# Two pairs of stores made one DMA each, and the last rows' x loaded in sixteen small DMAs on ScalarE's queue (dropout, adjacency product, layer norm, one Trainium2 core)

## What is computed

```python
def reference(x, adj, u):                       # x, u: (8192, 64); adj: (8192, 8192), fp32
    keep = (u >= 0.1).astype(x.dtype)
    x_drop = x * keep / (1.0 - 0.1)
    y = x + jnp.matmul(adj, x_drop)
    m = jnp.mean(y, axis=-1, keepdims=True)
    v = jnp.var(y, axis=-1, keepdims=True)
    return (y - m) / jnp.sqrt(v + 1e-5)
```

## Time and profile before

| | |
|---|---|
| median of 3 runs | 643.01 us (642.99 to 643.07) |
| the profiled execution | 643.25 us, its span 641.5 us |
| granted TensorE clock, mean | 0.927 of full speed |
| TensorE busy | 514.2 us, 80% of the span |
| VectorE, ScalarE, GpSimd busy | 48.6, 10.8 and 18.0 us |
| moved by DMA | 274.80 MB, mean 428 GB/s over the span |

### The profile page before, as it was taken

How to read it: one execution, slowest core, us unless ns; L and a number is a source line. 1 busy time by engine, 2 the same in 40 slices (tenths; PEclk the granted TensorE clock), 3 DMA queues, 4 the chain that set the end, 5 groups by cost and what they waited for, 6 DMA issues and landing times.

```text
span 641.5 us, 5637 instructions
## 1 busy us (share of the span) xinstructions
PE 514.2 (80%) x2308; PEld 175.9 (27%) x2308; DVE 48.6 (8%) x230; ACT 10.8 (2%) x18; POOL 18.0 (3%) x27
## 2 busy tenths in 40 slices
PE   0397888778988797797788779788797788689796
PEld 0132223222222232232232223222232232223225
DVE  2100101010010100101010010100001010000102
ACT  0000000000000000000000000000000000000000
POOL 0000000000000000000000000000000000000000
PEclk9998888998979798898989989798898989989999
DMA  9999999999999999999999999999999999999998
GB/s 374 423 448 436 429 432 440 416 440 425 430 436 450 412 449 440 429 426 443 413 440 429 430 432 454 426 432 443 423 430 439 420 437 447 428 416 428 434 422 335
DMA packets 9962, 274.80 MB, mean 428 GB/s; under 512 B 1388, under 2 KB 1642, under 8 KB 2666
## 3 DMA queue, kind: packets, MB, share of 16 engines
q1 hardware_dynamic: 9660, 274.60, 99.5%
q10 hardware_dynamic: 300, 0.16, 0.1%
HBM read 272.66 MB, written 2.10 MB: 428 GB/s over the span
## 4 chain that ended last, share of the span: by engine, by line
DMA 70%; PE 27%; issue 1%; SPq 0%; DVE 0%; POOL 0%; POOLq 0%; ACT 0%; DVEq 0%
DMA raw<-adj_dram 70%; PE acc L173 26%; SPq L132 0%; PE turned L193 0%; POOL rstd L268 0%; DVE stats L238 0%; POOLq L47 0%; ACT sums L211 0%; DVE rows L234 0%; SPq L137 0%; SPq L135 0%; SPq L136 0%; DVE moments L243 0%; POOLq L273 0%; DVE final_normed L261 0%
## 5 line engine op out<-in xcount | busy, mean ns | idle before, releaser
L173 PE MATMUL acc<-raw,dropped 128*64 128x504 f32 x2048 | 488.5, 637 | 93.3 <-POOLq L273 89.3
L173 PEld LDWEIGHTS acc<-raw,dropped 128*64 128x64 f32 x2048 | 152.9, 147 | 417.2 <-issue 291.5
L234 DVE TENSOR_TENSOR rows<-turned,x_sb 126x256 f32<-126x256 f32 x16 | 6.8, 425 | 541.8 <-PE turned L193 541.8
L268 POOL TENSOR_TENSOR rstd<-var_eps,minus_half 126x4 f32<-126x4 f32 x16 | 16.2, 1013 | 613.4 <-DMA raw<-adj_dram 330.2
L193 PE MATMUL turned<-join,sums 128*126 128x64 f32 x128 | 17.5, 279 | 10.9 <-ACT sums L211 10.9
L193 PEld LDWEIGHTS turned<-join,sums 128*126 128x126 f32 x128 | 15.3, 189 | 24.8 <-ACT sums L211 24.8
L211 ACT COPY sums<-acc 128x504 f32<-128x504 f32 x16 | 9.3, 579 | 616.3 <-PE acc L173 616.3
L249 DVE TENSOR_SCALAR normed<-rows,moments,rstd 126x64 f32 x64 | 15.7, 310 | 29.4 <-POOL rstd L268 29.4
L183 PE MATMUL final_turned<-x_final,eye 128*128 128x64 f32 x2 | 0.7, 449 | 18.1 <-DVE dropped L229 18.1
L238 DVE BATCH_NORM_STATS2 stats<-rows 126x6 f32<-126x64 f32 x64 | 9.7, 214 | 0.5
L173 PE MATMUL final_acc<-raw,dropped 128*64 128x128 f32 x128 | 7.3, 274 | 0.0
(11 more groups left out here) (14 smaller groups left out, 2.6 us busy)
## 6 DMA issues: line engine op xcount, KB each, us to landing
raw<-adj_dram SPq DMA_DIRECT2D x30, 5544.0 KB, 26.8
raw<-adj_dram SPq DMA_DIRECT2D x14, 5040.0 KB, 29.0
raw<-adj_dram SPq DMA_DIRECT2D x2, 3024.0 KB, 21.9
raw<-adj_dram SPq DMA_DIRECT2D x2, 2520.0 KB, 27.5
raw<-adj_dram SPq DMA_DIRECT2D x2, 2016.0 KB, 23.6
raw<-adj_dram SPq DMA_DIRECT2D x2, 1512.0 KB, 26.9
dropped<-u_dram SPq DMA_DIRECT2D x1, 2048.0 KB, 7.8
x_sb<-x_dram SPq DMA_DIRECT2D x1, 2048.0 KB, 12.3
```

The lines of the kernel that those rows point to most:

```text
L173: last = nc.tensor.matmul(sum_bank[t * D:(t + 1) * D, 0:width], dropped[:, t * PAIRS + q, :], raw[:, s, start:start + width], start=(q == ...
L234: nc.vector.tensor_tensor(rows[:, :, :], turned[0:ROWS, 0:GROUPS, :], x_sb[0:ROWS, bass.ds(b * GROUPS, GROUPS), :], ALU.add).then_inc(turn ...
L268: nc.gpsimd.tensor_tensor(rstd[:, :], var_eps[:, :], minus_half[0:ROWS, :], ALU.pow).then_inc(rstd_ready, 1)
```

## The change

The three edits are these.

1. Each pair of stores becomes one DMA of 126 partitions.
2. The one load of `x_final`, 128 rows on SyncE's queue ahead of the first slot, becomes sixteen DMAs on ScalarE's queue, of 1, 2, 3, ... 15 and then 8 rows of 256 bytes, all at ScalarE's start; TensorE waits for all sixteen.
3. The third slot of the block before the last one is loaded by one DMA in the ordinary loop, not by four.

```diff
-EVEN = ROWS // DMA * DMA
+FINAL_X = [*range(1, DMA), 8]
...
-        def store_blocks(engine, p0, p1, b0, b1):
-            engine.dma_start(out_dram[p0:p1, b0 * GROUPS * D:b1 * GROUPS * D],
-                             normed[p0:p1, b0 * GROUPS:b1 * GROUPS, :]).then_inc(blocks_stored, DMA)
+        def store_blocks(engine, b0, b1):
+            engine.dma_start(out_dram[:, b0 * GROUPS * D:b1 * GROUPS * D],
+                             normed[:, b0 * GROUPS:b1 * GROUPS, :]).then_inc(blocks_stored, DMA)
...
-            sp.dma_start(x_final[:, :], x[ROWS * CHUNKS:N, :]).then_inc(x_final_loaded, DMA)
...
-            with sp.Fori(1, BLOCKS - 2) as b:
+            with sp.Fori(1, BLOCKS - 1) as b:
...
-            for s in range(SLOTS - 1):
-                sp.wait_ge(multiplied, (BLOCKS - 3) * SLOTS + s + 1)
-                load_slot(BLOCKS - 2, s)
-            sp.wait_ge(multiplied, (BLOCKS - 2) * SLOTS)
-            for n, (s, q0, q1) in enumerate(PARTS):
-                if s == SLOTS - 1:
-                    load_part(BLOCKS - 2, n)
...
-            for p0, p1 in [(0, EVEN), (EVEN, ROWS)]:
-                store_blocks(sp, p0, p1, 0, BLOCKS - 1)
-            sp.wait_ge(blocks_stored, 4 * DMA)
+            store_blocks(sp, 0, BLOCKS - 1)
+            sp.wait_ge(blocks_stored, 2 * DMA)
...
-            pe.wait_ge(x_final_loaded, DMA)
+            pe.wait_ge(x_final_loaded, len(FINAL_X) * DMA)
...
             act.sem_inc(turned_free, 1)
+            row = 0
+            for n in FINAL_X:
+                act.dma_start(x_final[row:row + n, :], x[ROWS * CHUNKS + row:ROWS * CHUNKS + row + n, :]).then_inc(x_final_loaded, DMA)
+                row += n
...
-            for p0, p1 in [(0, EVEN), (EVEN, ROWS)]:
-                store_blocks(act, p0, p1, BLOCKS - 1, BLOCKS)
+            store_blocks(act, BLOCKS - 1, BLOCKS)
...
-            for s in range(1, SLOTS - 1):
+            for s in range(1, SLOTS):
                 pass_slot(BLOCKS - 2, s)
-            for n, (s, q0, q1) in enumerate(PARTS):
-                if s == SLOTS - 1:
-                    pass_part(n, 1)
-            for n, (s, q0, q1) in enumerate(PARTS):
-                pass_part(n, 2 if s == SLOTS - 1 else 1)
+            for n in range(len(PARTS)):
+                pass_part(n)
```

More of the change, by code:

```diff
@@ L105, in dropout_matmul_layernorm @@
         turned_free = semaphore("turned_free")
-        rows_ready = semaphore("rows_ready")
         stats_ready = semaphore("stats_ready")
@@ L273, in pass_slot, with pass_part @@
                 pool.sem_inc(landed, IN_SLOT[s])
-            def pass_part(n, loads):
-                pool.wait_ge(part_loaded[n], loads * DMA)
+            def pass_part(n):
+                pool.wait_ge(part_loaded[n], DMA)
                 pool.sem_inc(landed, 1)
```

## The result

| | before | changed |
|---|---|---|
| median of 8 runs | 642.99 us | 644.85 us |
| lowest to highest | 642.81 to 643.26 | 644.49 to 645.65 |
| span of the profiled execution | 641.5 us | 643.8 us |

The ratio is 1.003, with a 95% interval of 1.0021 to 1.0038: 1.9 us slower, where 643.4 and no change were forecast, and outside the range of 642.1 to 644.5. The profiled execution of the changed kernel was the slowest of its eight, 645.65 us; the spans of the others were 642.1 to 643.0.

The account below looks back on a forecast made before the run. The prediction took the DMA engines as the bound, the last to finish setting the end. Its terms, +0.61 - 0.14 - 0.09 + 0 = +0.38 us, gave 643.63 us profiled, a 643.4 us median, range 642.1 to 644.5 us.

Parts of the forecast that it names:

- x_final's: At the start, sixteen loads on ScalarE's queue land by 19 us at worst, while adj is still being loaded: 0 us.
- What bounds the kernel: Whole run: the DMA engines never run dry at 433 GB/s, and the engine that finishes last sets the end.
- Stores: Output stores: 14 engines store one row more on either queue, +0.61 us; fewer DMAs save 0.09 us.
- Merged loads: Block 14's third slot: one DMA in place of four saves three at 0.05 us each, -0.14 us.
- What merging uncovers: Blocks 14 and 15: TensorE finishes block 14's third slot 2.5 us later, block 15's waits cover it, 0 us.
- x_final's shares: x_final's load: the first engine gets 16 rows and 16 end packets, the last none; -0.15 to +0.25 us, taken as 0.
- the clock's: Last block: TensorE's clock falls after 618 us, the final store goes out 1.7 to 2.9 us later; 644.6 us, chance 0.08.
- the spared engine's: End of run: the last engine is one of the two with no added store row; 642.1 us, chance 0.12.
- The share of engines: Stores: far fewer engines share the rows, 14 rows on 9 engines, 3.7 us more, 646.5 us; chance 0.03.

Follow-up runs that it names:

- the run with fourteen DMAs: The changed kernel with x_final loaded by fourteen DMAs on ScalarE's queue, twelve of 8 rows and two of 16: 643.55 us, ratio 1.0008.
- product late: The changed kernel with TensorE's product of x_final and its wait moved behind the loop over the blocks, all sixteen DMAs kept: 643.47 us, ratio 1.0006.

## Why the prediction was wrong

**The step that failed** is x_final's: "Even with the 12.0 us to landing of the old load counted for the later ones, 19 us is the worst, and `adj` is still being loaded then; 0 us." TensorE's wait lasted until 38.2 us, and the `x_final` edit alone cost 1.56 us. The prediction took the landing time of a load that stood in the same queue as u and x for loads in a queue of their own. Each DMA engine takes packets from the two queues in turn. The engine with 16 rows and 16 end packets, which the prediction counted, has to let one packet of SyncE's queue pass for each of them but the first two, which started before that queue's first packet. The packets let pass took 0.6 us while u and x were loaded, and 1.6 us once `adj` was. The packet records of the changed kernel's trace show the turns: at the end of the sixteen loads, rows and end packets follow one another on an engine at 1.65 us, and each is followed at once by one packet of `adj` of 1.64 us. The prediction priced those 32 packets at their own 0.02 us. What counts is the packet that passes in between, 80 times as long.

The Trainium skill has this rule (DMA: Bandwidth & Descriptors, "Queues, rings and completion order"): an engine goes round the queues that have work, a packet at a time, and such a packet typically holds 9 to 17 pieces (descriptors). The trace agrees on the turns. It differs on the size: here a turn was a single row of 256 bytes or a single end packet. The prediction read that page for the shares and did not apply this rule. A row in the same page of the Trainium skill ("Rules for kernel authors") says that spreading DMAs over issuing engines does not help bandwidth and only saves issue time. The traces agree on bandwidth: outside the gap the rate is that of before. The row says nothing of the time to landing, and there the queue made the difference: sixteen loads were there by 18.05 us on SyncE's queue, and at 38.2 us on ScalarE's.

**The loss is a threshold, not a sum.** The prediction also had "The DMA engines never run dry", and at 51 us they did. In the loop it saw that "two other slots, 25 us of transfer, are queued meanwhile", and that is the cover for a late TensorE. At the start it was used up: 12 us of lateness (26.80 to 38.83) delayed the first reload from 39.52 to 51.30, and the queued slots ended at about 51. Lateness of 5.8 us, in the run with fourteen DMAs, stayed inside the cover. Past it the loss is not the excess alone. The reload was issued only some 0.3 us after the queued slots ended, and 2.3 us were lost: 0.96 us pass from the issue to the first packet, and the first packet on each engine was slow. That an empty queue has this price is shown by two traces; what makes the first packets slow is not. The prediction looked for TensorE's use of `x_final` but did not ask what a wait there would do to the queue.

**Point by point.**

- What bounds the kernel: right. The rate outside the one gap is that of before.
- Stores, +0.61 - 0.09: the shares are right (540 packets, and 284 in the run of the stores alone), the price was somewhat high: +0.34 by the stores alone, +0.43 between the run with these and the third-slot edit and that with the third-slot edit only (643.26 - 642.83, of different sets). Neither is clear of noise alone.
- Merged loads, -0.14: the medians say -0.20, and 0.15 us came back in the changed kernel's chain. The interval of the run alone takes in no change.
- What merging uncovers, 0 us: right in its effect. TensorE's pause was 2.4 us as worked out. The clock fell behind that pause in several runs, the changed kernel among them (0.74 from 589.2 to 592 us), which the prediction gave to a rival that would be costly only after 618 us. From 618 to 630 us the granted clock is 1.00 in every profile. The waits of block 15 absorbed the fall, as that rival's text allowed. (Its price has a slip: 1.7 to 2.9 us less the 0.9 us of cover are 1.4 us on the mean and not 1.2. No run tests it.)
- x_final's shares, -0.15 to +0.25, taken as 0: with no wait, the unequal shares were 0.21 (product late) and 0.30 us (SyncE's queue) over one load of 128 rows on SyncE's queue, the upper end, but neither is clear of noise. The second of these also has `adj` land later, so it is no clean price. That the last engine is one of those given more rows would explain both; no view here shows single engines, and it stays open.
- The rivals: the clock's and the spared engine's did not come about. The share of engines is settled by the packet counts. None of them named the wait for `x_final`.

The parts add up roughly: +1.56 (x_final alone) + 0.34 (stores) - 0.20 (third slot) = +1.70 us, against +1.86 measured for all three. Between single runs of the kernels with the wait until 38 us the times also vary more (643.99 to 646.3 for x_final alone, 642.68 to 643.49 for the kernel before beside it). The two traces of such kernels differ in TensorE's clock: its first record at full speed stands at 44.44 us in the changed kernel and at 42.73 us in the run with x_final alone, and the first reload went out at 51.30 and 50.37 us. Past the cover such a difference counts. That it makes the spread of the runs is not shown.

The third edit alone is the only version that came out under the kernel before, at 642.83 us. Its interval, 0.9987 to 1.0005, does not part the two.

## What to carry to other kernels

In a queue beside a stream of large packets, a small load waits one turn per packet on the engine that gets most of them, here 1.55 us each. So issue it ahead of the stream in the same queue, or as one DMA spread over all engines, or put its first use late; each of these gave back 1.3 to 1.6 of the 1.9 us, and the runs do not tell them apart. When a start is delayed, compare the delay with the transfers that are queued: up to that point it cost next to nothing here, and past it the empty queue cost the gap and some 0.8 us for slow first packets, for good, in a kernel that its transfers bound. And count a DMA's partitions against 16: by the packet counts one store of 126 uses 14 engines.

## What was not expected of the hardware

- Sixteen loads of 32 KB in all, beside a stream at 433 GB/s, needed until 38.2 us; the same bytes in one DMA on the same queue were there 8.0 us after their issue.
- A queue that ran empty did not start again at its full rate: the first packet of 44,352 bytes on each engine took 1.7 to 3.0 us in the changed kernel, and 1.64 us in the running stream.
- On ScalarE's queue the single load landed sooner (8.0 us) than behind u and x on SyncE's queue (12.0 us), as its rows pass between their packets.
